# Layer 0 of a two-layer decoder: feed-forward products issued inside a packed attention, and both normalisations along the free dimension

## The reference

```python
xn = layernorm(x)                                   # over the 512 features, no scale or bias
q, k, v = heads(xn @ w_q.T), heads(xn @ w_k.T), heads(xn @ w_v.T)      # 32 heads of 16
attn = softmax(q @ k.T / 4) @ v                     # 512 queries x 512 keys, 2 batches
gate = (xn @ gate_w.T) * gate_scale                 # 1376 inner features
up = (xn @ up_w.T) * up_scale
ffn = ((silu(gate) * up) @ down_w.T) * down_scale
x = x + merge(attn) @ w_o.T + ffn
xn = layernorm(x)                                   # input of layer 1
```

## Time and profile before

| | us |
|---|---|
| time, median of 3 runs (lowest to highest) | 2384.16 (2381.96 to 2385.5) |
| the profiled execution | 2379.31 |
| its span, first to last instruction | 2377.6 |

### The profile page before, as it was taken

The page is one execution under the profiler, slowest core; times in us unless marked ns, Lnnn a source line. Parts: engine busy times, 40 slices in busy tenths (PEclk is TensorE's granted clock), DMA queues, the critical chain, the costliest instruction groups (busy, mean ns, idle before and its releaser), DMA issues. The chain is left out here.

```text
span 2377.6 us, 36518 instructions
## 1 busy us (share of the span) xinstructions
PE 2219.5 (93%) x12008; PEld 1631.4 (69%) x12008; DVE 1489.7 (63%) x1755; ACT 1334.6 (56%) x2339; POOL 847.7 (36%) x724
## 2 busy tenths in 40 slices
PE   5989999999599999989999899899899995999998
PEld 3744444888377777767777677677677764888886
DVE  4466662741557877768768586777687754555555
ACT  2245554320248778667877777777678763322322
POOL 3100000000025676657556565666575662000000
PEclk8989999999799999999999999999999997999999
DMA  2633432220134455444544444454445555544462
GB/s 81 193 65 61 69 57 69 88 88 24 67 111 135 142 180 164 141 145 137 166 134 149 149 149 147 140 168 137 145 134 162 163 186 184 185 141 137 144 206 83
DMA packets 177294, 310.60 MB, mean 131 GB/s; under 512 B 18785, under 2 KB 90977, under 8 KB 176881
## 3 DMA queue, kind: packets, MB, share of 16 engines
q1 hardware_dynamic: 177136, 308.52, 43.6%
HBM read 252.52 MB, written 55.68 MB: 130 GB/s over the span
## 5 line engine op out<-in xcount | busy, mean ns | idle before, releaser
L141 PE MATMUL ssm_pp<-xhi,ssm_lo 128*128 128x512 f32 x1192 | 487.8, 409 | 38.4 <-issue 25.9
L143 PE MATMUL ssm_pp<-xhi,ssm_hi 128*128 128x512 f32 x1192 | 472.0, 396 | 0.0
L142 PE MATMUL ssm_pp<-xlo,ssm_hi 128*128 128x512 f32 x1192 | 470.4, 395 | 0.0
L1268 ACT ACTIVATE ssm_sct<-ssm_cumb,ssm_gpar 128x128 f32<-128x128 f32 x1024 | 313.0, 389 | 106.8 <-DMA ssm_cumb<-dt_sums 97.4
L141 PEld LDWEIGHTS ssm_pp<-xhi,ssm_lo 128*128 128x128 f32 x1192 | 227.2, 191 | 104.4 <-issue 47.3
L1369 DVE SCALAR_TENSOR_TENSOR ssm_xc<-ssm_pp,vectors,ssm_xc 128x1022 f32<-128x1022 f32 (+2 forms) x192 | 245.1, 1277 | 47.7 <-ACT ssm_xc L1229 32.9
L133 POOL TENSOR_TENSOR ssm_lo<-ssm_raw,ssm_hi 128x512 fp32r<-128x512 f32 x146 | 246.6, 1695 | 62.3 <-ACT ssm_hi L122 62.3
L143 PEld LDWEIGHTS ssm_pp<-xhi,ssm_hi 128*128 128x128 f32 x1192 | 227.1, 190 | 53.3
L1404 DVE TENSOR_TENSOR ssm_sct<-ssm_sct,ssm_cbm 128x1024 f32<-128x1024 f32 x128 | 228.8, 1788 | 48.8 <-ACT ssm_sct L1275 48.7
L142 PEld LDWEIGHTS ssm_pp<-xlo,ssm_hi 128*128 128x128 f32 x1192 | 227.6, 191 | 45.8
L1416 DVE TENSOR_TENSOR ssm_xp<-ssm_turn,ssm_gpar 128x512 f32<-128x512 f32 x128 | 87.7, 686 | 246.8 <-PE ssm_turn L1124 239.7
(11 more groups left out here) (210 smaller groups left out, 4093.2 us busy)
## 6 DMA issues: line engine op xcount, KB each, us to landing
ssm_cumb<-dt_sums SPq DMA_DIRECT2D x96, 1024.0 KB, 6.5
ssm_raw<-w SPq DMA_DIRECT2D x149, 256.0 KB, 2.7
gated<-ssm_go SPq DMA_DIRECT2D x128, 256.0 KB, 5.3
out_graw<-gated SPq DMA_DIRECT2D x64, 512.0 KB, 4.2
out_raw<-w SPq DMA_DIRECT2D x65, 256.0 KB, 2.7
ssm_cumb<-dt_sums SPq DMA_DIRECT2D x32, 512.0 KB, 4.5
ffn_raw<-w SPq DMA_DIRECT2D x37, 256.0 KB, 2.7
stk_qs<-qk_parts SPq DMA_DIRECT2D x48, 128.0 KB, 3.8
```

The costliest lines, as they stand in the source:

```text
L141: pe.matmul(out, wlo, xhi, start=start, stop=False)
L142: pe.matmul(out, whi, xlo, start=False, stop=False)
L143: return pe.matmul(out, whi, xhi, start=False, stop=stop)
L1268: i = act.activation(sct[:, s % 2, h, :], cumb[:, s % 2, 0, h, :], ACT.Relu, scale=-1.0, bias=gpar[:, unit, 0, s % NTOK, h:h + 1])
```

## The change

Layer 0 keeps its mathematics and changes its layout and order:

- The input comes with tokens on partitions (8 tiles of 128x512). The first norm takes mean and variance by `bn_stats` and `bn_aggr` along the free dimension, scales, and PE transposes the result (32 transposes).
- Each head takes 48 partitions instead of 96 where it did matmuls before (the three rows of 16, two heads in the two halves of 64 partitions); a pair of `row_step` or of `key_step` matmuls addresses the two halves. `pv` takes all four column groups at once and is issued 4 times a step instead of 8. The scores' PSUM buffer for the maximum is single (`deep` 1) instead of double.
- The 528 gate and up matmuls are issued inside attention, 4.5 after each sub-step in the first three quarters and 3 in the last. Silu becomes Tanh with arithmetic on DVE, and h stays in float32.
- The down projection comes first, then the output projection, both with tokens on partitions (h and the attention are the stationary side). The high and low parts of h are made two tiles at a time, just ahead of PE.
- The second norm is taken token tile by token tile as the output projection ends, with 64 transposes (32 for the norm, 32 for the residual stream).

```diff
-KSTACK = 96
+KSTACK = 48
@@ emit_first_norm (in place of emit_layernorm "ln0")
+            def moments(t):
+                dve.wait_ge(x_in[t], 16)
+                dve.bn_stats(stats[:, t, :], x[:, t, :]).then_inc(stats_done, 1)
+                dve.wait_ge(stats_done, t + 1)
+                dve.bn_aggr(mv[:, t, :], stats[:, t, :]).then_inc(var_done, 1)
+            def normalise(t):
+                dve.wait_ge(std_done, t + 1)
+                dve.reciprocal(rs[:, t:t + 1], rs[:, t:t + 1]).then_inc(rstd_done, 1)
+                dve.wait_ge(rstd_done, t + 1)
+                dve.tensor_scalar(x[:, t, :], x[:, t, :], mv[:, t, 0:1], rs[:, t:t + 1], ALU.subtract, ALU.mult
+                                  ).then_inc(normed, 1)
+            def low(t):
+                dve.wait_ge(hi_done, t + 1)
+                dve.tensor_tensor(xlo[:, :, tokens(t)], ps[:, t % slots, :, :],
+                                  xhi[:, :, tokens(t)].bitcast(F32), ALU.subtract).then_inc(lo_done, 1)
...
@@ Stacks
+            for half in range(2):
+                src = c.qk_rows[part, side, bass.ds(r + half * 2 * DK, 2 * DK), i % 2 * L:(i % 2 + 1) * L]
+                at = half * HALF + row * DK
+                sp.dma_start(dst[at:at + DK, i, :, :].bitcast(F32),
+                             src.rearrange("(h d) t -> d h t", h=2)).then_inc(self.stacked[i], 16)
...
+        after(pe, self.max_done, n * 8 + (u - deep + 1))
+        for half in range(2):
+            at = slice(half * HALF, half * HALF + KSTACK)
+            mm = pe.matmul(rows[:, u % deep, half, :], self.qs[at, i, u // 4, qt * P:(qt + 1) * P],
+                           self.ks[at, i, u // 4, :], start=True, stop=True)
@@ emit_attention, SP and POOL
+            feed.begin_load(sp)
+            for n in range(feed.begun, 5):
+                feed.load(sp, w, W_FFN + n, 0, n)
             sweep(sp, body)
...
+            feed.begin_lo(pool)
             sweep(pool, body)
@@ emit_attention, PE: one step
                     for k in range(8):
+                            st.row_step(pe, rows, *step(it, i, 2), k, 1)
+                        key_step(it, i, 2 * k)
+                        key_step(it, i, 2 * k + 1)
+                        if k == 1 and not (last and i == NB - 1):
                             turn(*step(it, i, 1))
...
+                        if k in (2, 4, 6):
+                            pv(it, i, k // 2 - 1)
+                        for m in products(i * 8 + k, last):
+                            gate_up(it, m)
@@ emit_attention, ACT: between exps(2k) and exps(2k+1)
+            def events(it, kk, last):
+                for nn, b in ended(kk, last):
+                    if nn % 2 == 0:
+                        gate(it, nn, b)
+                    if b == 0:
+                        feed.split_hi(act, it * (2 * PER), nn + 2, it * (2 * PER // feed.raw_slots) + (nn + 2) // feed.raw_slots)
@@ emit_down (in place of emit_ffn's second half and emit_layernorm "ln1"), ACT
+            def h_high(k):
+                after(act, tile_done, FIRST + k - 1 if k >= 2 else 0)
+                act.activation(h_hi[:, k % 2, :], h[:, k, :], ACT.Copy).then_inc(h_hi_done, 1)
...
+            for k in range(FT):
+                if k + 1 < FT:
+                    h_high(k + 1)
+                if k + 2 < FT:
+                    feed.split_hi(act, 0, FIRST + k + 2, (FIRST + k + 2) // feed.raw_slots)
+                elif k + 2 < FT + KT:
+                    o_high(k + 2 - FT)
+                if k in (2, 4, 6, 8):
+                    a_high(k // 2 - 1)
@@ DVE
+            for k in range(FT):
+                if k + 1 < FT:
+                    h_low(k + 1)
+                if k in (1, 3, 5, 7):
+                    invert(k // 2, 0)
+                if k in (2, 4, 6, 8):
+                    invert(k // 2 - 1, 1)
+                    divide(k // 2 - 1)
+                if k in (3, 5, 7, 9):
+                    a_low(k // 2 - 1)
...
+            for t in range(NTOK):
+                add(t)
+                if t >= 1:
+                    low(t - 1)
+                scale(t)
+            low(NTOK - 1)
@@ PE
+            for t in range(NTOK):
+                for k in range(KT):
...
+                    mm = product(pe, ps[:, t, :], a_hi[:, k, tokens(t)], a_lo[:, k, tokens(t)],
+                                 o_hi[:, k, :], o_lo[:, k, :], False, k == KT - 1)
+                mm.then_inc(summed, 1)
+                if t >= 1:
+                    turn_norm(t - 1)
+                if t >= 2:
+                    turn_sum(t - 2)
+            turn_sum(NTOK - 2)
+            turn_norm(NTOK - 1)
+            turn_sum(NTOK - 1)
```

More of the change, by code:

```diff
@@ L204, in _ @@
         @block.tensor
         def _(pe):
[L206 to L218, removed]
+            for t in range(NTOK):
+                pe.wait_ge(normed, t + 1)
+                after(pe, lo_done, t - slots + 1)
+                for k in range(KT):
+                    mm = pe.transpose(ps[:, t % slots, k, :], x[:, t, k * P:(k + 1) * P], c.ident[:])
+                mm.then_inc(turned, 1)
@@ L240, in _ @@
+            feed.begin_hi(act)
         @block.vector
         def _(dve):
[L242 to L251, removed]
@@ L271, in over_partitions @@
+            for t in range(NTOK + 2):
+                if t < NTOK:
+                    moments(t)
+                if 1 <= t <= NTOK:
+                    normalise(t - 1)
+                if t >= 2:
+                    low(t - 2)
+            feed.begin_lo(dve)
 def over_partitions(rows):
@@ L517, in out, with weights @@
                                      ).then_inc(out_moved[i % 2], 16)
+            def weights(it, i, last):
+                for k in range(8):
+                    for nn, half in ended(i * 8 + k, last):
+                        if half == 0:
+                            feed.load(sp, w, W_FFN + tile(it, nn + 5), it * (2 * PER), nn + 5)
             def body(it, last):
@@ L609, in body @@
             def body(it, last):
                 for i in range(NB):
-                    if not (last and i >= NB - 2):
-                        for u in range(2):
-                            st.maximum(dve, rows, *step(it, i, 2), u)
-                    if i > 0:
-                        out(it, i - 1)
-                    elif not isinstance(it, int) or it > 0:
-                        out(it - 1, NB - 1)
-                    if not (last and i >= NB - 2):
-                        for u in range(2, 4):
-                            st.maximum(dve, rows, *step(it, i, 2), u)
@@ L730, in _ @@
[L730 to L734 removed]
+                pe.wait_ge(h_lo_done, k + 1)
+                q = n % feed.slots
+                for t in range(NTOK):
+                    mm = product(pe, ps[:, t, :], h_hi[:, k % 2, tokens(t)], h_lo[:, k % 2, tokens(t)],
+                                 feed.hi[:, q, :], feed.lo[:, q, :], k == 0, False)
```

573 lines of the change are left out of this document (309 added, 264 removed).

## The result

The changed kernel takes 2282.49 us, the median of 4 runs (2281.85 to 2285.25), beside 2383.70 for the kernel before in 4 runs on the same chip (2381.96 to 2385.50): 0.9573 of the time, 95% interval 0.9559 to 0.9588. The forecast was 2275, range 2246 to 2320. The profiled execution took 2281.85, with a span of 2279.9.

The account below looks back on a forecast made before the run. PE was taken to bound attention, gate and up, and waiting chains the norms; -15 (first norm) + 1 (q, k, v) - 89 (attention, gate, up) - 5 (down, output, second norm) = -108 us on 2379.31, median 2275, range 2246 to 2320.

Parts of the forecast that it names:

- x: In each attention sub-step, PE's way between full and half array and back: taken as 0.15 us, between 0 and 0.31.
- `pv`'s round trip: In attention before the change, switching between `pv` and the other matmuls and back: 0.31 us, 0.15 per change.
- my own sum for attention: PE's work per sub-step in attention with gate and up, 2.27 us for 96 sub-steps, less in the last quarter: 276 us.
- ACT's meetings: In attention, Tanh and split meet between two exponentials 11 times and delay a key matmul, 0.65 us each: 7 us.
- attention over 300 us: Sign of being wrong: attention with gate and up, forecast at 283 us, taking under 255 or over 300.
- Packing: In attention, row and key pairs run side by side, 0.235 us a pair; rivals: rows in turn 0.09, no gain 0.04.
- One price for the tables: In attention, exponential and Tanh switch without table loads, cost 0; the rival with loads, 2320 us, had chance 0.03.
- My terms: First norm: start, first input, eight token tiles, last tile's chain, first weights; ending at 29 to 30 us, 15 saved.
- q, k, v: Projection stage: SP's longer queue against some tenths saved by packed row matmuls; +1 us, between -3 and +5.
- The recurrence: Down projection followed tile by tile: first matmul at 2.4, DVE's 11.5 us per two tiles against PE's 11.0, end at 70.
- the 5 us that I laid on top for clock and POOL: Down projection: 3 us for the cold clock at its start and 2 for POOL slowing DVE, making 75 us.
- the 3 allowed: Layer 1, forecast unchanged at 1737 us; moving by over 3 us would show the prediction wrong.

Follow-up runs that it names:

- the first experiment: Changed kernel with only the order of heads altered, so both key matmuls of a pair use the same array half: 2305.04 us, 0.9662 of the kernel before.

## Why the prediction was right, and by which step it was off

**The step that missed: x, the way between full and half array and back.** It was taken as 0.15 us per sub-step, between 0 and 0.31. Measured are 0.40 in a sub-step without `pv` (0.096 ahead of the row pair and 0.104 behind it, 0.096 ahead of the first gate product and 0.103 behind it) and 0.20 in one with it (the first two): 0.30 in the mean, the upper bound. The bound was right, since it took over `pv`'s round trip, and the choice inside it was wrong. `pv`'s own round trip came out as read: 0.10 ahead of it, 0.11 behind it and 0.10 behind the first gate product make the 0.31.

With x = 0.30 my own sum for attention, 276 us, becomes 276 + 128 x 0.15 = 295, and with the 7 us of ACT's meetings 302; measured are 302.7. Smaller misses cancel in that. In the last quarter PE waits for buffers, some 4 us: a mean sub-step takes 2.19 with the row matmuls and 1.99 without, where the terms with x = 0.30 give 2.08 and 1.84 (without `pv`, the row pairs there stand 1.83 apart; in the stretch without row pairs the second matmul of every other key pair waits, seen as 0.83 instead of 0.40 for the pair). Against that, the mean sub-step before it is 2.41 and not 2.42, ACT's meetings cost some 6 us and not 7 (1.7 of them in the very first sub-step), and the 302.7 leave out the end of the last sub-step. The rest of the 20.6 us lies around attention: its start was 1.3 us shorter than forecast and its end 2.5 longer.

**The sign of being wrong was there.** I had named attention over 300 us as one, and it took 302.7: by my own measure the sum for attention failed, though the total lay inside the range.

**Luck in the total.** The forecast, 2275, is 7.5 us off. On the profiled execution the miss is 10.5: attention gave 20.6 us less and the other stages 10.3 more. Then the median lay 0.6 us above the profiled execution and not 4.85, which took 4.2 of the miss away again, and my last sum was 1.2 short (2379.31 - 108 + 4.85 is 2276.2).

**What bounds attention** was right: PE is busy in 303.27 of 305.50 us. Packing was right, by the starts 3 or 4 ns apart and by the first experiment. One price for the tables was right too: there is no table load between exponentials and Tanh.

**The first norm.** My terms, 4.06 + 2.7 + 16.5 + 3 + 2.7, make 28.96, and the norm ended at 28.92. That is 24.9 us, and I had rounded it up to 26 and then to 15 saved: the 1.9 us that it saved beyond that were lost in the rounding and not in a cost. The period per token tile was 2.36 us for 2.3, with costs that were off both ways. In the timeline of the kernel after:

```profile
14.12 0.69 DVE L226 BATCH_NORM_STATS2 ln_stats<-stk_v 128x6 f32<-128x512 f32 x1
...
15.10 0.55 DVE L234 TENSOR_SCALAR stk_v<-stk_v,ln_mean_var,ln_rstd 128x512 f32<-128x512 f32 x1
```

The statistics cost 0.69 (0.65 taken) and the scaling 0.55 (0.37 taken, half of a pass of 1024 with one operation); DVE's waits on itself were shorter than the 0.25 taken.

**q, k, v.** +1 forecast, -1.7 measured, with the clock at 1.00 instead of 0.96: PE's one long wait in the stage was 2.4 us instead of 4.5, and the clock did not fall behind it. With the norm alone that wait was 5.7 and the stage 85.7, though SP issues no more there than before; what SP's longer queue costs is therefore shown by no run. The start of attention cost 1.2 us more instead of 2.5.

**Down, output, norm.** The recurrence holds: the first matmul at +2.4, and DVE's low parts of h at 457.38, 471.10, 484.39 and 497.67, 13.72 and 13.29 apart, where I had 13.6 for two tiles. Of the 5 us that I laid on top for clock and POOL, 2 came: 72.1 instead of 75. They are the clock's: the first tile took 7.89 us, with matmuls 0.43 apart until 440.0, and a later one 5.44. Without them my 70 us were 69.7, and no cost of POOL is left to be seen. Output and norm took 39.8 for 41, 3.6 us a tile for 3.95.

**Layer 1** moved by 1.6 us, inside the 3 allowed. In other kernels it took 1732.4 to 1739.2 us with the same instructions, so a few us of a difference between single executions are no one's doing.

## What to carry over

- Packing two short-contraction matmuls side by side saved one matmul's time per pair, 0.23 us here, and each change between full and half array took 0.2 of it back, half of it ahead of the first matmul of the new kind and half behind it. Count the changes in the order of instructions, and put packed pairs next to each other: two pairs with a change in and one out gained 0.06 us, with `pv` in place of the change out 0.28.
- Where an engine executes in order, a copy that needs a late result holds all behind it: one tile later in the order was worth 6 to 8 us here. Look for the long idle time of an unloaded engine whose next instruction had its input long before.
- After a large change of PE's order look at the granted clock first: with less work in the gate and up products the kernel was 31 to 90 us slower.

## What was not expected of the hardware

- With packed pairs and little dense work between them, the granted clock was 0.56 over 384 us, and PE worked without a pause for 108 and for 75 us at the lower level before the full clock came back; with dense products between them, or with unpacked pairs, it was 0.99.
- A change between full and half array shows on both sides of the first matmul behind it: 0.096 us ahead and 0.104 behind. Eight `pv` matmuls of 32 columns take 1.00 us, from the first start to the next kind of matmul.
- Whether POOL slowed one of DVE's passes of 1024 depended on which of the two began first. In the down projection a low part of h begun 0.56 us ahead of POOL's subtraction took 1.22 us (471.10 and 471.66), as alone; the low part of the attention begun 0.58 behind one (498.81) took 2.31, where it takes 1.16 alone. With ACT's copy a tile later one low part of h began 0.10 ahead of POOL and took 1.22, while POOL took 2.27 instead of 1.29, and another began 0.15 behind POOL and took 2.33. So the order on the two engines decides which one pays.
